# Queries gathered by three bf16 one-hot matmuls, and one running maximum for each block of four pairs, in a graph attention layer

## What is computed

```
q = (x @ Wq + bq).reshape(N, H, D);  k, v the same way
e = (angle_emb @ We).reshape(-1, H, D)
k_e = k[src] + e
v_e = v[src] + e
alpha = einsum('ehd,ehd->eh', q[dst], k_e) / sqrt(D)
a = exp(alpha - segment_max(alpha, dst)[dst])
attn = a / segment_sum(a, dst)[dst]
out = segment_sum(attn[:, :, None] * v_e, dst).reshape(N, H * D)
x_r = x @ Wskip + bskip
beta = sigmoid(concatenate([out, x_r, out - x_r]) @ Wbeta)
out = layernorm(beta * x_r + (1 - beta) * out) * ln_gamma + ln_beta
result = layernorm(x + x + relu(out))
```

## Time and profile before

| | us |
|---|---|
| median of 3 runs | 2606.56 |
| lowest and highest run | 2601.0, 2606.98 |
| profiled execution, first to last instruction (its span) | 2124.7 |
| median less span | 481.9 |

### The profile page before, as it was taken

One profiled execution on the slowest core, in us unless ns is written; L12 is line 12 of the kernel. 1 busy time (PEld: TensorE's weight loads), 2 busy tenths in 40 slices (PEclk: granted clock), 3 DMA queues, 4 the chain that ended last, 5 costly groups with the idle time before them and its releaser, 6 DMA issues. The chain is left out here.

```text
span 2124.7 us, 43320 instructions
## 1 busy us (share of the span) xinstructions
PE 1580.3 (74%) x10903; PEld 1429.2 (67%) x10903; DVE 1807.1 (85%) x3704; ACT 1121.3 (53%) x3755; POOL 1502.4 (71%) x1586
## 2 busy tenths in 40 slices
PE   7678788778776777777776777777777777877763
PEld 5577777668676666666675776667666767767652
DVE  6687787788878888888888898898898999999985
ACT  1154445445445545555555555566555665666656
POOL 0377777777777777777777777777777777777750
PEclk9898899998999999999999989999999999899985
DMA  8887787777777777777777777777777777777741
GB/s 297 280 246 233 233 240 235 236 233 236 222 215 212 218 216 214 222 211 218 221 215 225 216 223 217 222 226 221 215 223 225 226 224 228 224 226 219 228 128 36
DMA packets 298207, 467.63 MB, mean 220 GB/s; under 512 B 49766, under 2 KB 192826, under 8 KB 297862
## 3 DMA queue, kind: packets, MB, share of 16 engines
q1 hardware_dynamic: 222552, 259.24, 39.7%
q0 software_dynamic: 75408, 205.58, 33.7%
HBM read 413.96 MB, written 50.66 MB: 219 GB/s over the span
## 5 line engine op out<-in xcount | busy, mean ns | idle before, releaser
L742 POOL DMA_INDIRECT kv<-kv_tab,src_all x1498 | 1425.4, 952 | 480.9 <-issue 443.4
L851 PE MATMUL e_ps<-we,ea 128*128 128x128 f32 x3136 | 472.2, 301 | 278.4 <-DVE kve L1437 271.8
L851 PEld LDWEIGHTS e_ps<-we,ea 128*128 128x128 f32 x3136 | 417.7, 208 | 324.5 <-DVE kve L1437 175.6
L1437 DVE TENSOR_TENSOR kve<-kv,e_ps 128x768 f32<-128x768 f32 (+1 forms) x392 | 421.6, 1084 | 214.8 <-DMA kv<-kv_tab,src_all 214.0
L1095 ACT ACTIVATE dist_en<-iota_n,neg_rel 128x128 bf16<-128x128 f32 x1568 | 500.0, 396 | 46.3 <-issue 46.3
L1119 ACT ACTIVATE wt_ps<-logit,used_b 128x64 f32<-128x64 f32 x196 | 62.3, 318 | 831.3 <-issue 692.0
L969 PE MATMUL sum_ps<-wv,hot_en 128*128 128x136 f32 x3136 | 466.4, 303 | 11.8 <-DVE wv L1487 4.6
L969 PEld LDWEIGHTS sum_ps<-wv,hot_en 128*128 128x128 f32 x3136 | 429.7, 209 | 31.9 <-issue 31.9
L864 PE MATMUL q_ps<-q_win,hot_ne 128*128 128x128 f32 x3136 | 420.6, 292 | 0.9 <-DMA q_win<-q_tab 0.9
L864 PEld LDWEIGHTS q_ps<-q_win,hot_ne 128*128 128x128 f32 x3136 | 407.3, 210 | 1.2 <-DMA q_win<-q_tab 1.2
L1458 DVE TENSOR_REDUCE logit<-prod 128x64 f32<-128x1024 f32 x196 | 239.2, 1220 | 19.4 <-issue 0.4
(11 more groups left out here) (144 smaller groups left out, 1237.9 us busy)
## 6 DMA issues: line engine op xcount, KB each, us to landing
ea<-eaT SPq DMA_DIRECT2D x196, 512.0 KB
row_b<-rel_row SPq DMA_DIRECT2D x196, 256.0 KB
q_win<-q_tab SPq DMA_DIRECT2D x392, 64.0 KB
kv<-kv_tab,src_all POOLq DMA_INDIRECT x1498
sum_tab<-sums SPq DMA_DIRECT2D x391, 59.5 KB
kv_tab<-tab_buf SPq DMA_DIRECT2D x33, 384.0 KB, 3.7
logit<-sum_tab SPq DMA_DIRECT2D x49, 136.0 KB
xt_buf<-xT SPq DMA_DIRECT2D x33, 192.0 KB, 4.0
```

Of the source, the lines that this page charges most:

```text
L742: pool.indirect_dma_start(out=head_rows(q) if u == t == 0 else kv[:, s, t, :], out_offset=None, in_=kv_tab[:, :], in_offset=bass.IndirectO ...
L851: mm = pe.matmul(e_ps[u][:, t * P:(t + 1) * P], ea[:, par, (u * TILES_G + t) * P:(u * TILES_G + t + 1) * P], we[:, :], start=True, stop=True)
L1437: dve.tensor_tensor(kve[:, s, a:TILES_G, :, :], kv[:, s, a:TILES_G, :].rearrange("p t (a c) -> p t a c", a=2), e4[:, a:TILES_G, :, :].to_b ...
```

## The change

**Maximum for blocks.** The path of the maximum is taken once for a block of four pairs (`BLOCK = 4`) and not for each pair. In the last step of a block DVE reduces all four slots of `ring` at once (`top_out`, 256 numbers a partition); PE transposes at the end of the next step, DVE takes it into the running maximum a step later (`running_max`), PE spreads it a step after that, and ACT copies it to four columns of `used_b` one more step later, for the block that follows.

**Queries in bf16.** `q_tab` has three bf16 rows in the place of a float32 one: the high part, the part of what is left, and the rest, 768 bytes a node against 512. `hot_ne` and `q_win` are bf16. `q_spread` does three accumulating matmuls a tile. To make the parts, ACT rounds (`query_high`, `query_middle`) and DVE subtracts (`query_rest`, `query_low`), once for the twelve early blocks, at the start, and once for each build, one and two steps later. SP's store of a build (`store_queries`) moves from behind the load of the query windows to behind the stores of the sums.

```diff
-                sp.wait_ge(qrow_ev, r - Q_AHEAD + 1)
+                sp.wait_ge(qleft_ok, 2 * (r - Q_AHEAD) + 5)
...
                 for t in range(TILES_G):
-                    mm = pe.matmul(q_ps[u][:, t * P:(t + 1) * P], hot_ne[:, 2 * par + u, t * P:(t + 1) * P],
-                                   q_win[:, 2 * par + u, :], start=True, stop=True)
+                    for k in range(Q_PARTS):
+                        mm = pe.matmul(q_ps[u][:, t * P:(t + 1) * P], hot_ne[:, 2 * par + u, t * P:(t + 1) * P],
+                                       q_win[:, 2 * par + u, k * C:(k + 1) * C], start=(k == 0), stop=(k == Q_PARTS - 1))
...
-                if spread:
-                    max_spread(q - LAG + 1, 1 - par, q - 1, q - LAG + 1)
-                if top:
-                    top_row(q - 1, 1 - par, min(max(q - LAG + 2, 1), PAIRS - LAG))
+                if q % BLOCK == 2 and BLOCK < q <= PAIRS - BLOCK:
+                    max_spread(q // BLOCK)
+                if q % BLOCK == 0:
+                    top_row(q // BLOCK)
...
-                if first is None and q > LAG:
-                    maximum_out(q - LAG, slice(q, q + 1))
+                if q % BLOCK == BLOCK - 1 and BLOCK < q < PAIRS - BLOCK:
+                    maximum_out(q // BLOCK, slice(q + 1, q + 1 + BLOCK))
...
-                pair_top(q, par, reuse)
-                if first is None or first >= 3:
-                    pair_max(q - 2, par, q - 3 if first is None else None)
+                if q % BLOCK == BLOCK - 1:
+                    top_out(q // BLOCK + 1, ring[:, :, :].rearrange("p r c -> p (r c)"), 2 * q + 2)
+                if q % BLOCK == 1 and q > BLOCK:
+                    running_max(q // BLOCK, q // BLOCK - 1)
+                if q - 2 in build:
+                    query_low(build[q - 2])
+                if q - 1 in build:
+                    query_rest(build[q - 1])
                 weighted(q, par, reuse)
...
+            act.wait_ge(qleft_ok, 1)
+            act.copy(ahead3[:, :, :, 0, :], q_ahead[:, :, :, :]).then_inc(qcast_ok, 1)
...
+            dve.wait_ge(qcast_ok, 1)
+            dve.tensor_tensor(q_ahead[:, :, :, :], q_ahead[:, :, :, :], ahead3[:, :, :, 0, :], ALU.subtract
+                              ).then_inc(qleft_ok, 1)
...
+            dve.wait_ge(qcast_ok, 2)
+            dve.tensor_tensor(ahead3[:, :, :, 2, :], q_ahead[:, :, :, :], ahead3[:, :, :, 1, :], ALU.subtract
+                              ).then_inc(qleft_ok, 1)
```

More of the change, by code:

```diff
@@ L647, in _ @@
                         store_first(q - 4)
+                    if q - 4 in build:
+                        store_queries(build[q - 4])
                     if q == PAIRS + 4:
@@ L971, in node_sums, with step @@
                 mm.then_inc(sum_ok, 1)
-            def step(q, par, i, sums=True, first_use=False, last=False, top=True, spread=True):
+            def step(q, par, i, sums=True, first_use=False, last=False):
                 if sums:
@@ L1331, in table_rows @@
                     if r < Q_ROUNDS:
-                        dve.tensor_tensor(q_ahead[:, r, b, :], bank[:, 2 * C:3 * C], b_kvq[:, 2 * C:3 * C], ALU.add)
+                        last = dve.tensor_tensor(q_ahead[:, r, b, :], bank[:, 2 * C:3 * C], b_kvq[:, 2 * C:3 * C], ALU.add)
+                        if r == Q_ROUNDS - 1 and b == TB - 1:
+                            last.then_inc(qleft_ok, 1)
                     dve.tensor_tensor(tab_buf[:, r % TSLOTS, b, :], bank[:, 0:2 * C], b_kvq[:, 0:2 * C], ALU.add
                                       ).then_inc(tab_ev, 1)
-            for r in range(7):
+            for r in range(6):
+                table_rows(r)
+            dve.wait_ge(qcast_ok, 1)
+            dve.tensor_tensor(q_ahead[:, :, :, :], q_ahead[:, :, :, :], ahead3[:, :, :, 0, :], ALU.subtract
+                              ).then_inc(qleft_ok, 1)
+            for r in range(6, 7):
                 table_rows(r)
@@ L1684, in _ @@
             with dve.Else():
+                for r in range(Q_AHEAD, Q_UNITS):
+                    query_rest(r)
+                    query_low(r)
                 dve.memset(spread[:, 0:2], BIG).then_inc(wide_steps, 2)
```

174 lines of the change are left out of this document (109 added, 65 removed).

## The result

| | before | after |
|---|---|---|
| median | 2603.78 us (4 runs, 2596.04 to 2606.98) | 2567.26 us (4 runs, 2564.53 to 2575.39) |
| ratio | 1 | 0.9882, 95% interval 0.9849 to 0.9915 |
| profiled execution, first to last instruction | 2124.7 us | 2567.8 us |

In this comparison the change makes the kernel 1.2% faster, clear of 1 but small; I had forecast no change. The median moved by 36 us, while the span of the profiled execution went up by 443 us. The time of the profiled execution of after is 2569.63 us, 1.8 us more than its span. So the 481.9 us between span and median, which I had carried along as a constant, are no constant.

The account below looks back on a forecast made before the run. The prediction took POOL's gathers, never idle for a reason, to bound the loop. It summed 2606.6 + 1.3 (start) + 0 (loop) - 0.5 (end) = 2607.4 us, range 2450 to 2640, likeliest case 2603.6 to 2615.4.

Parts of the forecast that it names:

- The failed step: Whole-kernel time: the 481.9 us by which the median exceeds the profiled span were carried along unchanged.
- the loop adds 0: Main loop: all added work hides under POOL's gathers at 10.05 us a step; 0 us, bounds -1 and +3.
- Rival A: Loop: timed executions go at PE's pace, at a lower clock, so faster, 2254 us at one end; chance 0.26.
- B: Loop: transfers set the pace, 3.4% more bytes cost at most 83 us, so 2690 us; chance 0.08.
- C: Loop: DVE's `hot_ne` in bf16 keeps POOL from writing descriptors, +119 to +238 us, some 2725; chance 0.03.
- D: Loop: PE's block gets longer and its clock falls, PE exceeding POOL's 10.05 us; +190 us at clock 0.6; chance 0.03.
- DVE: DVE's work per loop step: early steps from 8.0 to 8.3 us, late ones from 9.5 to 9.0, under 10.05.
- PE: PE's work per loop step: 7.8 us becomes between 6.8 and 8.4; query block 1.5 to 2.9 us.
- DMA: Loop transfers: 16 MB more, 3.4%, at a share of 0.74 to 0.80; hidden even at 0.83.
- ACT: ACT's work per loop step: two more copies in 44 steps, from 4.9 to 5.7 us, hidden.
- The start: Table building before the first gather: transfers add 1.3 us, DVE's 3.5 us hidden; bounds 0 and +4.8.
- The sum: Whole kernel: 2606.6 + 1.3 + 0 - 0.5 = 2607.4 us, with the bounds of its terms 2603.6 to 2615.4.

Follow-up runs that it names:

- second kind: Group of two chips in the follow-up runs, on which the unchanged kernel before took 2119.78 and 2120.51 us.
- first kind: Group of three chips in the follow-up runs, on which the unchanged kernel before took 2534.53, 2533.31 and 2529.91 us.
- after with constants: Kernel after, window numbers fixed in the program instead of read by SP: 2128.72 us (1.0054) on the second kind, 2495.67 us (0.9862) on the first kind.
- block maximum with constants: Kernel before with only the maximum for blocks of four, window numbers fixed in the program: 2119.03 us, ratio 0.9998, on the second kind.
- one matmul a tile: Kernel after with only the first of three bf16 matmuls per query tile: 2128.37 us (1.0044) on the second kind, 2484.15 us (0.981) on the first kind.
- the chip of the first heading: First-kind chip that ran before unchanged (2535.43 us), the maximum for blocks alone (2489.44), bf16 queries alone (2616.83) and after (2521.62).
- 16 rows: Kernel after, third and fourth gather of each group fetching 16 rows, not 128: 2078.02 us (0.9806) on the second kind, 2530.67 us (1.0004) on the first kind.
- the run with the pause: Kernel before with the maximum for blocks, POOL also waiting mid-step for its first group's gathers to land: 2578.21 us, 1.2157, second kind.

## Why the prediction was wrong, point by point

**The failed step** is the one that the prediction called its weakest: "I make the sum against 2606.56 and carry the 481.9 us along unchanged." The trace was of an execution with a step of 10.05 us, as the second kind of chip shows. The timed ones were of the first kind, whose step measured 12.05 us on another chip. (2606.56 - 2124.7) / 196 is 2.46 us; the gap before the first gather measured 2.33 - 0.31 = 2.02 us a step there, where the difference between the medians of the two kinds is 414 us. (The result's own before has no trace at its pace.) All that the prediction hid under POOL's cover was hidden under a POOL that never waits. In the timed executions POOL waits for PE in each step, so PE's block counts and the term "the loop adds 0" doesn't hold. The whole change gave -10 to -13 us on three chips of this kind and -36 us in the result, against a forecast of +0.8.

**Rival A** was right that PE is in the path, wrong in how. It took the clock for the reason (16 records at 3.75 us). The clock is lower (0.778), but a block that isn't caught is short: 1.45 us for 23 records in the timeline above. What is late is the issue of a few instructions and the rise of `q_ok`. Its prices were wrong for that reason. The maximum, taken at 0.9 us a step, gives a gap that is 0.16 us shorter, and 41 to 45 us in the medians, not 176. The query block, taken at -0.9 us a step within -0.9 to +1.9, costs 0.43 (82 to 86 us).

**Rivals B, C and D.** B: the DMA share after is 0.61 to 0.64, under that of before, at 3.5% more bytes; not seen. C: `hot_ne` takes 1213 ns as before and the gathers 950, so what the rival feared of `hot_ne` isn't seen; but the two subtractions of a build do lengthen gathers, by some 4 us in all (below). D: the lower clock came (0.78 mean), on both kernels of the first kind alike; on the second kind one at 0.82 and one at 0.91 make the same 160 gathers.

**The steps of the sum, where they can be judged** (after with constants, second kind, which has all of the change but SP's reads of window numbers). Its stretches of 300 to 500 and 1700 to 1900 us, for the earlier trace rows:

```profile
300.00:500.00 200.00, 145.16 (x1222) 135.56 (x1222) 161.77 (x233) 105.57 (x345) 151.52 (x160) 0.88 0.78 245
1700.00:1900.00 200.00, 142.15 (x1207) 131.60 (x1207) 181.77 (x374) 123.74 (x407) 151.54 (x160) 0.89 0.78 231
```

Its gathers (durations min/median/max, first and last start), those of the block maximum with constants on the same chip, two of its query blocks in the timeline, and one gather beside the subtractions of a build:

```profile
L758 POOL DMA_INDIRECT kv<-kv_tab,src_all x1498: 942/946/2234, 84.1 to 2046.3; - x188
```

```profile
L744 POOL DMA_INDIRECT kv<-kv_tab,src_all x1498: 942/946/1578, 81.5 to 2037.2; - x188
```

```profile
1206.09 2.77 PE L881 MATMUL q_ps<-q_win,hot_ne 128*128 128x128 bf16 x24
...
1215.37 1.50 PE L881 MATMUL q_ps<-q_win,hot_ne 128*128 128x128 bf16 x24
```

```profile
233.11 0.41 DVE L1557 TENSOR_TENSOR tab_buf<-tab_buf 128x256 bf16<-128x256 f32 x1
...
233.18 1.50 POOL L758 DMA_INDIRECT kv<-kv_tab,src_all  x1 [0.30 <-issue]
...
233.45 0.40 DVE L1551 TENSOR_TENSOR tab_buf<-tab_buf 128x256 f32<-128x256 f32 x1
```

- *DVE*: 161.8 x 10.02 / 200 = 8.1 us early and 9.1 late; forecast 8.3 and 9.0. The reduction of 256 numbers: 420 ns, as forecast. Right.
- *PE*: 7.3 us a step; forecast between 6.8 and 8.4. The block of 24 bf16 records takes 1.50 us; 1.5 was the lower of my two ends; another, at a lower clock, takes 2.77. Right for this kind.
- *DMA*: share 0.78; bound 0.83. Right. *ACT*: 105.6 x 10.02 / 200 = 5.3 us; forecast 5.7.
- *The loop*: from the first gather to the last 1962.2 us, as in the profiled before (another chip). The block maximum on the same chip has 1955.7, so the term of 0 was some 6 us too low, over its upper bound of 3. The gaps add up to the same in both (476 us); the gathers themselves are longer. Of the 376 gathers of steps 2 to 48, 69 overlap one of the two new subtractions on DVE, and these last 1008 ns on average where the others last 946: 4 us. By this overlap it is what rival C feared, from another operation and at a small price; no run took the subtractions out alone. That the gathers' data would not hold POOL back was right.
- *The start* was mis-sized. The first gather is at 84.1 us (85.3 with one matmul a tile), against 81.5 in the block maximum on the same chip and 79.8 in the profiled before: +2.6 to +5.5 where I took +1.3, and on the chip of the first heading +6 to +8 (83.1 and 84.5 us with the bf16 queries, 76.7 and 77.3 without). Between traces of one chip it can differ by several us without a reason that I know (84.8 to 90.5 on the third). The prediction said that near 85 would mean that DVE was the bound there. POOL's wait for DVE's `bad` before it is 48.8 and 50.0 us in the two, 46.5 in the block maximum with constants: most or all of the two subtractions (3.5 us by my sum) is paid, and they weren't hidden.
- *The sum* on the second kind: +8.9 us measured (2128.72 - 2119.78), +0.8 forecast. Between the traces of after and of the block maximum, both with constants, the start gives +2.6, the loop +6.4 and the end -2.6 us. The remaining 2 to 3 us of the medians aren't explained.

For a bf16 matmul with its weight load the rule that the prediction quoted from the Trainium skill (TensorE: Matmul & The Clock Gate, "Back-to-back issue gap") gives some 81 ns, 1.94 us for the block. The trace has 1.50 us for 24 of them, 62 ns each; the measurement decides, and the block alone is a gain of 0.45 us here, as half a float32 record would give. It didn't help: on one kind of chip POOL doesn't wait for it, on the other it is caught.

**What stays open.** First, what delays PE's and SP's issue and the rise of `q_ok` on some chips. The runs exclude SP's register reads (constants) and the gathers' bytes (16 rows) as its cause. They show one thing that goes with it without exception: the thirteen traces with the stretches hold 12,700 to 17,300 records of semaphores, the seven without them 55,700 to 57,100, of much the same programs. Most of those that are missing tell of the landing of a DMA (9,000 to 12,400 against 48,300 to 49,000); the engines' own are 3,500 to 4,900 against 7,300 to 8,300, and those of `q_ok` are nearly all there in both. So the recording of the execution is incomplete there, and it may be what holds the engines, or the same unknown cause may do both. The Trainium skill (NOTIFIC — the notification-queue block, "7.1 Overflow: three behaviours, one of which stalls the engine") says that the block which writes such records always holds its sources back inside rather than lose one there, and that a full ring drops the new record, overwrites the oldest or stalls the engine. No trace here shows which of these was set. No run here had recording off, so this wasn't tested, and then part of the 414 us might not exist without it. Second, whether the gap on the first kind goes when POOL doesn't wait for `q_ok`; the run for it met the other kind. So did the run with the pause, and with it rival G, that PE's reports come late until POOL pauses, stands untested. Third, why the result's comparison gave 0.9882, when three others on the first kind gave 0.9950 to 0.9957.

## What to carry to other kernels

Compare the span of the profiled execution with the median before anything else is read. Where they differ by much more than here on one and the same execution (1.8 us), the trace is likely to be of another pace than the times, and a bound that is read from it has to be argued at both paces; work that is free under one engine's cover may be on the path at the other. When an engine's waits stand at "issue" or "remote" while the releaser's matmuls are long over, look for how late its semaphore rises, and count the instructions it has to issue up to there: on the first kind of chip here eight more matmul records a step (24 bf16 ones for 16 float32 ones), with as many more weight loads, cost more than their shorter time gave. Check too which rise the wait needs: the last one before the waiting instruction may be of a later block. Of a change with two parts, time each alone: on the first kind the better kernel was half of it (0.982 and 0.983 against 0.995), on the second the block maximum with constants gave nothing (0.9998).

## What the runs showed of the hardware

- The same program takes 2120 us on two chips and 2530 to 2535 on three, with at most 0.6% between the fastest and the slowest execution on each.
- On the slower ones PE and SP start one instruction per 0.70 or 1.40 us for part of each step (in before, its two parts and after PE 274 to 652 us of an execution, SP 1147 to 1475 us); DVE, ACT and POOL have next to none of them, and their waits end when these do.
- There the semaphore of a query block rose 0.2 to 9 us after the start of its last matmul (median 0.3 to 7.6 by kernel), against 0.2 to 0.4 us on the others.
- An indirect gather of 128 rows holds POOL for 946 ns, one of 16 rows for 852 to 859: its time is nearly all fixed.
- A gather that ran beside a DVE subtraction of two tensors in SBUF (256 numbers a partition, 0.41 us) took 1008 ns on average, and up to 1500, against 946 (after with constants, second kind, 69 and 307 gathers).
- A bf16 matmul of 128 columns with its weight load takes 62 ns in a row of 24, a float32 one 244 ns (two records of the 1.95 us for 16).
